# Cross-attention softmax of a decoder layer: one exponential per head with bias and sum output, in place of a subtraction on GpSimd and a sum on VectorE

## The reference

```python
energy = jnp.einsum('bhqd,bhkd->bhqk', Q, K) * scale          # scale = 1/4, 77 keys, 16 heads
energy = jnp.where(m == 0, -1000000000.0, energy)
attn = jax.nn.softmax(energy, axis=-1)
out = jnp.einsum('bhqk,bhkd->bhqd', attn, V)
...
return out @ Wo + bo
```

## Time and profile before

| | |
|---|---|
| Time, median of 3 runs | 884.16 us (883.88 to 889.25) |
| Profiled execution, time | 888.0 us |
| Profiled execution, span of its records | 886.2 us |
| PE, DVE, ACT, POOL busy | 87%, 71%, 52%, 34% of the span |

### The profile page before, as it was taken

The page is one execution under the profiler, slowest core; times in us unless marked ns, Lnnn a source line. Parts: engine busy times, 40 slices in busy tenths (PEclk is TensorE's granted clock), DMA queues, the critical chain, the costliest instruction groups (busy, mean ns, idle before and its releaser), DMA issues.

```text
span 886.2 us, 14985 instructions
## 1 busy us (share of the span) xinstructions
PE 771.1 (87%) x4736; PEld 382.2 (43%) x4736; DVE 630.2 (71%) x1098; ACT 459.1 (52%) x920; POOL 303.3 (34%) x252
## 2 busy tenths in 40 slices
PE   6789999999999899999988798988599999999910
PEld 3442222222322222222223566565458777777710
DVE  2588888888788886888856865759637444688657
ACT  2226777777777676777776525152424344435400
POOL 8001500000000895920024645455712554543321
PEclk9889999999999999999999987979699999999965
DMA  7746030310404798860000900000131322412121
GB/s 197 189 93 155 1 91 19 75 34 20 78 13 90 238 263 256 268 173 1 1 1 0 375 4 1 1 0 25 54 121 53 108 86 82 147 53 79 55 97 47
DMA packets 48515, 80.76 MB, mean 91 GB/s; under 512 B 16116, under 2 KB 35063, under 8 KB 47289
## 3 DMA queue, kind: packets, MB, share of 16 engines
q1 hardware_dynamic: 35017, 45.43, 18.7%
q0 software_dynamic: 9952, 31.29, 11.1%
q10 hardware_dynamic: 3472, 3.08, 1.5%
HBM read 48.21 MB, written 33.11 MB: 92 GB/s over the span
## 4 chain that ended last, share of the span: by engine, by line
PE 63%; DVE 17%; DMA 5%; POOL 5%; issue 5%; ACT 3%; SPq 1%; DVEq 0%; POOLq 0%; ACTq 0%
PE bank L533 11%; PE bank L525 11%; PE quad L506 10%; PE quad L835 9%; PE bank L849 6%; DVE rowmax L911 6%; PE bank L632 3%; PE quad L603 3%; PE bank L457 2%; ACT probs L1370 2%; POOL sc L1648 2%; DMA kstack<-k_parts 1%; PE quad L678 1%; POOL sc L1643 1%; DMA qstack<-q_parts 1%
## 5 line engine op out<-in xcount | busy, mean ns | idle before, releaser
L911 DVE TENSOR_REDUCE rowmax<-quad 128x1 f32<-128x1024 f32 x256 | 302.8, 1218 | 74.5 <-PE quad L506 73.8
L1370 ACT ACTIVATE probs<-bank 128x512 f32<-128x512 f32 x512 | 284.0, 595 | 115.7 <-PE bank L525 113.1
L525 PE MATMUL bank<-qstack,kstack 98*128 98x512 bf16 x512 | 194.3, 388 | 11.7 <-ACT probs L1370 10.0
L506 PE MATMUL quad<-kstack,qstack 96*128 96x512 bf16 x512 | 177.7, 387 | 15.0 <-DVE rowmax L911 7.2
L533 PE MATMUL bank<-probs,v_all 128*32 128x512 f32 x1024 | 138.7, 610 | 0.0
L525 PEld LDWEIGHTS bank<-qstack,kstack 98*128 98x128 bf16 x512 | 48.9, 97 | 190.9 <-ACT probs L1370 162.8
L835 PE MATMUL quad<-xbT,w_all 128*128 128x128 bf16 x1104 | 99.8, 224 | 9.4 <-issue 5.7
L835 PEld LDWEIGHTS quad<-xbT,w_all 128*128 x1104 | 76.2, 97 | 34.4 <-issue 18.6
L506 PEld LDWEIGHTS quad<-kstack,qstack 96*128 96x128 bf16 x512 | 48.4, 99 | 76.4 <-DVE rowmax L911 39.9
L1689 POOL DMA_INDIRECT y_tokens<-ysb,dest x46 | 48.7, 1058 | 95.0 <-DVE ysb L1135 89.2
L1481 ACT ACTIVATE xbT<-bank 128x512 bf16<-128x512 bf16 x46 | 27.4, 597 | 95.6 <-PE bank L816 84.7
(11 more groups left out here) (168 smaller groups left out, 973.0 us busy)
## 6 DMA issues: line engine op xcount, KB each, us to landing
w_all<-w_split SPq DMA_DIRECT2D x2, 4096.0 KB, 18.3
xb<-x_sorted SPq DMA_DIRECT2D x46, 129.0 KB
x_sorted<-blank POOLq DMA_DIRECT2D x6, 774.0 KB, 8.3
w1raw<-in_w POOLq DMA_DIRECT2D x8, 512.0 KB, 5.9
w2raw<-in_w POOLq DMA_DIRECT2D x8, 512.0 KB, 5.6
w_split<-w1two POOLq DMA_DIRECT2D x8, 512.0 KB, 4.8
w_split<-w2two POOLq DMA_DIRECT2D x8, 512.0 KB, 3.2
q_parts<-parts SPq DMA_DIRECT2D x24, 128.0 KB
```

The costliest lines, as they stand in the source:

```text
L506: mm = pe.matmul(bank[2 * (p % 2) + e], q, kstack[slot][0:MAXROW, j, e * 512:e * 512 + 512], start=True, stop=True)
L525: mm = pe.matmul(bank[4 + i % 2], kstack[slot][0:KROWS, j, kt * P:kt * P + P], qstack[slot][0:KROWS, half, j, :], start=True, stop=True)
L911: dve.tensor_reduce(rowmax[:, k % 2, p:p + 1], quad[:, 2 * (p % 2):2 * (p % 2) + 2, :].rearrange("p a n -> p (a n)"), AX_X, ALU.max).then_ ...
L1370: act.activation(probs[:, i % PR, :], bank[4 + i % 2], ACT.Exp, scale=INV4).then_inc(probs_ready, 1)
```

## The change

The maximum of each head is multiplied by -1/4 on DVE (a new instruction over 16 elements, into the new tile `neg2`, semaphore `s2_negated`). `exp2` becomes 16 exponentials over 77 elements each, one per head, with that head's `neg2` as bias and the head's sum as a second output into `sum2`. The subtraction on POOL (`shift`) and the sum on DVE are gone. Nothing else is moved.

```diff
@@ take
                 dve.tensor_reduce(max2[:, n % SR, :], sc2[:, n % SR, :, :], AX_X, ALU.max).then_inc(s2_max, 1)
+                dve.wait_ge(s2_max, n + 1)
+                dve.tensor_scalar(neg2[:, n % SR, :], max2[:, n % SR, :], -INV4, None, ALU.mult).then_inc(s2_negated, 1)
@@ sum_probs
                 dve.wait_ge(p2_exp, n + 1)
-                dve.tensor_reduce(sum2[:, n % SR, :], sc2[:, n % SR, :, :], AX_X, ALU.add).then_inc(s2_summed, 1)
-                dve.wait_ge(s2_summed, n + 1)
                 dve.reciprocal(inv2[:, n % SR, :], sum2[:, n % SR, :]).then_inc(s2_recip, 1)
@@ exp2
-                act.wait_ge(s2_shifted, n + 1)
-                act.activation(sc2[:, n % SR, :, :], sc2[:, n % SR, :, :], ACT.Exp, scale=INV4).then_inc(p2_exp, 1)
+                act.wait_ge(s2_negated, n + 1)
+                for h in range(H):
+                    ex = act.activation(sc2[:, n % SR, h, :], sc2[:, n % SR, h, :], ACT.Exp, bias=neg2[:, n % SR, h:h + 1], scale=INV4,
+                                        accum_out=sum2[:, n % SR, h:h + 1])
+                ex.then_inc(p2_exp, 1)
@@ gpsimd
-            def shift(n):
-                pool.wait_ge(s2_max, n + 1)
-                sc = sc2[:, n % SR, :, :]
-                pool.tensor_tensor(sc, sc, over_heads(max2[:, n % SR, :]), ALU.subtract).then_inc(s2_shifted, 1)
-
...
-            shift(0)
-            shift(1)
             divide(0)
-            shift(2)
             divide(1)
...
-                if n + FAR < NT:
-                    shift(n + FAR)
```

More of the change, by code:

```diff
@@ L200, in build @@
         max2 = sb2("max2", [P, SR, H])
+        neg2 = sb2("neg2", [P, SR, H])
         sum2 = sb2("sum2", [P, SR, H])
@@ L238, in build @@
         q2_ready, q2_done = sem("q2_ready"), sem("q2_done")
-        s2_ready, s2_taken, s2_max, s2_shifted, p2_exp = map(sem, ("s2_ready", "s2_taken", "s2_max", "s2_shifted", "p2_exp"))
-        s2_summed, s2_recip, p2_done, p2_turned, pT_done = map(sem, ("s2_summed", "s2_recip", "p2_done", "p2_turned", "pT_done"))
+        s2_ready, s2_taken, s2_max, s2_negated, p2_exp = map(sem, ("s2_ready", "s2_taken", "s2_max", "s2_negated", "p2_exp"))
+        s2_recip, p2_done, p2_turned, pT_done = map(sem, ("s2_recip", "p2_done", "p2_turned", "pT_done"))
         o2_ready, o2T_done = sem("o2_ready"), sem("o2T_done")
```

## The result

The changed kernel took 909.56 us (median of 4 runs, 900.21 to 911.31) beside 884.24 us before: a ratio of 1.0265, 95% interval 1.0189 to 1.0342. In a second comparison, with more rounds, the ratio was 1.0257 (1.0219 to 1.0294). The change costs 2.6%, some 23 us. The single runs differ with PE's clock: its mean over the run was 0.948 in the one of 900.21 us and 0.933 to 0.937 in the other three. The profiled execution of the changed kernel took 911.3 us with a span of 909.5 us, 23.3 us more than that of before.

What follows compares the result with a forecast made beforehand. No engine was taken to hold the chain for long; the order of the queues sets a group's length. Opening 12.7, two groups 9.6, last group 3.5 and clock 4 gave 29.8 us on 884.2: 914 us, range 895 to 938.

Steps and rivals of the forecast that it cites:

- The price of a tile's exponentials: ACT's 16 exponentials of one cross-attention tile: 5.6 us in place of 1.23, with ends 4.0 and 9.0.
- The dear and the free rivals: ACT's sum output: dear, 933 or 952 us in all, chance 0.22; free, 892 to 898 us, chance 0.14.
- The group's replay: A full cross-attention group from the copy at 568.14, retimed at 5.6 us a tile: 4.8 us longer, two groups 9.6.
- The opening: 470 to 523 us, from the last self-attention unit: the first group's value matmuls start 12.7 us late.
- the clock: PE's granted clock falls to half behind long pauses in the opening: 4 us, with 0 and 10 as ends.
- the second pause: PE's pause made by `exp2(1)` in the opening, 4 us, after one of some 3.3 us made by `exp2(0)`.
- The end: The last group, 613 to 651 us: the logits start 3.5 us later.
- The slope: Cost of each further us of a tile's exponentials: 2.5 us in a group, 2.1 in the last; 11.1 in all.
- The faster rival: Handovers through POOL and DVE go, ACT works in idle time: 14 us less, 870 us, chance 0.05.

Runs made afterwards that it cites:

- the repetition: The changed kernel, unaltered, run again with more rounds on one chip and compared with the kernel before: 906.61 us, ratio 1.0257.
- the run with bias alone: The changed kernel without the sum output: 16 exponentials a tile with bias, the sum again on DVE; 897.78 us, ratio 1.0196 to the kernel before.
- the spread runs: The changed kernel with tiles 0 and 1's exponentials taken two heads behind each of score steps 17 to 31: first 907.10 us, then 903.22 us.
- the half sums: The changed kernel with the sum output on every second head only: 899.65 us, ratio 1.0194 to the kernel before.
- the filler alone: The kernel before with `turn_x2`'s eight transposes done four times, ahead of PE's pause: 876.38 us, ratio 0.9916.
- the cut alone: The kernel before with its exponential cut into 16, without bias or sum output; subtraction and sum stay: 898.05 us, ratio 1.0152.
- the run with one maximum: The changed kernel with one maximum per token over all heads as bias of one exponential, sum on DVE: 877.94 us, ratio 0.9891 to the kernel before.

## Why the prediction was right

914 us was forecast and 909.56 measured, with the range at 895 to 938. The mechanism, ACT's queue with its longer work per tile, is what the runs show. The sum was too high: 29.8 us were forecast, and the medians give 25.3, the stretch 23.0 and the repetition 23.5. Point by point:

**The price of a tile's exponentials** was put at 5.6 us, between 4.0 and 9.0. It was 5.6 for the first tile. The sum's output is a separate instruction of 190 ns that overlaps like ACT's others and adds 0.095 us a head, against the 0.10 taken from ACT's smallest instruction; the bias adds 0.09 and a bare piece costs 0.16 (2.62 us for 16). The dear and the free rivals fell with that. By an estimate from the page "ScalarE: Activation LUTs" of the Trainium skill, section "What ACT_TABLE_LOAD costs", a tile without sum output would have taken 4.1 us; the run with bias alone shows 4.09.

**The group's replay** held from `exp2(11)` on. Moved by 17.49 us, the distance of the two starts of the copy, it said 603.5 for the start of `exp2(11)`, 609.1 for its end and 611.0 for the logits. `exp2(10)`, which it had at 595.2, started at 595.69; the query copies behind it made that up. In ACT's and PE's timelines the later steps stand at:

```profile
603.53 0.37 ACT L1376 ACTIVATE sc<-sc,neg 128x77 f32<-128x77 f32 x1
...
609.00 1.09 ACT L1420 ACTIVATE wqkv<-bank 128x512 f32<-128x512 f32 x2
```

```profile
610.76 3.37 PE L679 MATMUL quad<-wg,wqkv 128*128 128x8 f32 x16 [3.82 <-DVE sc L1015]
```

The group as a whole cost 3.8 and 3.0 us and not 4.8. One term was left out: the clock in the later scores. The first four matmuls of `scores2(14)` in the third group took 2.39 us before, at the half clock, and I had carried that over. Now they take 1.27:

```profile
621.83 1.27 PE L604 MATMUL quad<-kbd,q2T 128*128 128x308 f32 x4 [2.53 <-DVE logits L1052]
```

With the four behind them and the scores ahead this accounts for 1.6 us of the third group's 1.8. In the second group it is the logits: they kept PE for 3.28 us to the start of the scores before and for 2.42 now, because the clock was still full at their start. That is 0.9 us of the 1.0 that were missing. First the kernel before, then the changed one:

```profile
543.95 3.42 PE L678 MATMUL quad<-wg,wqkv 128*128 128x8 f32 x16
```

```profile
562.09 2.57 PE L679 MATMUL quad<-wg,wqkv 128*128 128x8 f32 x16 [1.05 <-DVE sc L1015]
```

**The opening** was 12.7 us without the clock, and it measured 12.7. That includes the clock, which I had put at 4 us on top. This is the term that was most mis-sized, and the 4 us had no working behind them: the prediction's own reading was 5 to 10 us, and it took 4. The pause of 3.16 us (3.3 forecast) and the clock of 0.50 for ten us behind it came as described, but the second pause, forecast at 4 us, was 0.79, because PE's slower matmuls ran under `exp2(1)`. The self-attention unit ended 6.9 us late, against 6.1 without any clock. In the repetition's trace the clock was back at full by 482 us and the second pause was longer:

```profile
487.43 1.69 PE L526 MATMUL bank<-qstack,kstack 98*128 98x512 bf16 x3 [2.81 <-ACT probs L1371]
```

There the unit ended 8.2 us late, and still the first copy came only 12.3 us late. What the clock alone costs in the opening stays open: the spread runs take away the pause and the half clock together.

**The end** was put at 3.5 and cost 3.6 us.

**The slope**, 11.1 us for each us of a tile, was tested by the half sums: 0.75 us less gave 10.3 us in the trace and 6 by the ratios, 8 to 14 for a full us.

**The faster rival** said that the removals are worth 14 us if ACT's work doesn't grow. That was shown, and it was more: 19.5 us. Its price lacked the clock, which in the groups of the kernel before fell behind PE's pause of 2.9 us; the filler alone gave 4.7 and 5.8 us in two groups. The rule of the Trainium skill that speaks against many small pieces, on the page "VectorE: DVE Perf Modes", section "The TRN2 errata — SBUF-src ops pay a fixed extra latency per instruction", agrees with the runs: the cut alone, without bias and sum, adds 1.4 us to a tile and is already slower than before. It is a part of the loss; bias and sum output add another 3.0 us to a tile.

## What to carry to other kernels

Price an instruction that is cut into pieces by what each piece costs in an unbroken row, most of it a fixed part (here 0.16 us for 77 elements without bias, 0.25 with it, 0.34 with a sum as well) and by where the pieces stand in the queue: ACT was 52% busy, and still about a third of the 67 us added to it came out in the time, because the pieces stand between copies that others await. A removed pass is worth what is late next, and a good part of its worth can lie in the clock: look at the pause of PE that it shortens and at the clock behind it. When a sum output or a bias forces one instruction per head, look first whether the softmax needs a maximum per head, or one at all.

## What was not expected of the hardware

The clock held its full level behind the pauses of 0.3 to 0.7 us ahead of the third group's transposes, and was at half behind those of 2.9 and 3.2 us. Between them the traces show both: half behind 2.17 us in the run with one maximum, full behind 2.53 us in the changed kernel and behind 2.66 us in the run with the filler (1.00 from 512 to 518 us). A short pause is no surety either: in the first spread run no pause from 475 to 488 us was over 0.8 us, and the clock was 0.50 from 489 to 491. So the length of the last pause alone does not tell the level. Useless transposes in the pause, 2.6 us in each of three groups, made the kernel 6.8 us faster. ACT's read of a sum takes 190 ns in its row and adds only 0.095 us to a run of pieces.
